# Merging the experts' lists on 64 rows of batch and expert, in parts around the last block's gate

## The chip, the cores and the metric

One core of a Trainium2 chip runs one program that holds an attention layer and a layer of experts (MoE). The metric is the time of the program on the device in microseconds, the median of several executions. Nothing else runs on the core.

## What is computed

The input x has two batches of 2048 tokens with 256 features (float32). The reference is, cut to what matters here:

```python
x = x + attention(layernorm(x))      # 16 heads, segments of 64 tokens, a memory carried over segments
h = layernorm(x)                     # all 4096 tokens of both batches in one list
scores = sigmoid(h @ gate_w.T)       # 32 experts; 4 groups of 8, the best 2 groups stay
topk_idx, topk_w = best 4 of (scores + gate_bias) within those groups, weights normalised, times 2
# expert e takes the first CAP = 64 tokens that chose it, in the order of the list
h1 = silu(buf @ w1) * (buf @ w3);  ob = h1 @ w2
y = sum over the kept choices of weight * ob
x = x + y + shared(h)                # a shared expert on all tokens
```

The point for this change is the capacity. Of the 4096 tokens, each expert keeps only the 64 that come first. The kernel finds them as the 64 largest of a list: for each expert a row holds, at a token's place, N minus its number if the token chose the expert and 0 if not. The largest values are the earliest tokens.

## The kernel before, in words

The attention part goes through 16 blocks (`NBLK`) of 128 tokens of both batches, and in each through 4 groups (`NG`) of 4 heads. The order of the work on each engine is written out by hand, engine by engine, with semaphores between them; an engine works its own list strictly in that order. While block n + 1 is in attention, the rows of block n are finished: the output projection (`project_out`, L1591), the residual (`residual`, L1033), the second layer norm (`x1_stats`, `x1_newton`, `x1_apply`, L921 to L946), the transposes of the normed rows (`x1_transposes`, L1601), the logits (`logits`, L1609), the gate on VectorE (`gate_scores` to `gate_weights`, L1055 to L1114), the transposes of the picks (`pick_transposes`, L1615) and their product with the descending numbers `desc` (`picks`, L1119 to L1135), which yields for every expert a row of 128 values for each batch.

The rows of the first 14 blocks go out to memory and come back as `first_picks`: 128 rows (batch, half, expert) of 896 columns. `earliest` (L1142, L1143) takes the 64 largest of each of those rows in eight rounds. A round is one MAX8, which finds the eight largest of a row, and one MATCH_REPLACE8, which puts -1 in their places. Its result `first_kept` is four lists of 64 for each expert.

After the last block of attention the rest of the lists is merged on VectorE:

- The four lists of `first_kept` are copied side by side into `mid` (L1300), on 32 rows (one for each expert), and SP is told (`lists_kept`). Behind them lie the picks of block 15, both batches: 4 x 64 + 2 x 128 = 512 columns. `picks(15)` puts them there in two instructions (L1126), one for each batch.
- Eight rounds of `top8` (L1201, L1202) put the 64 largest of the 512 into the first 64 columns of `last_picks`.
- Then comes the last block: residual, layer norm, gate, picks. `picks(16)` puts its rows behind them: 64 + 256 = 320 columns.
- Eight rounds of `top8` on the 320 columns give `sel`, the final list. Between the rounds stand some sums of the shared expert (`shared_add`, L1195, and `shared_mul`, L1189).
- Three small steps (L1335 to L1339) make token numbers of it. TensorE turns them (`pair_tokens`, L1674), VectorE makes the indices (L1341), and POOL (GpSimd) gathers the experts' tokens with them (L653), stores and broadcasts the list to all partitions (L646, L676).

TensorE fills this stretch with the shared expert. Its order after the attention is:

```python
        attended_transposes(NT - 1)
        project_out(NBLK, NT)
        shared_half(0, 1, 0)
        shared_half(0, 1, 1)
        x1_transposes(NBLK)
        logits(NBLK)
        shared_down(0)
        shared_up(1, 0)
        pick_transposes(NBLK)
```

and then `shared_up(1, 1)`, `shared_up(2, 0)`, `shared_down(1)`, `shared_up(2, 1)`, `shared_up(3, 0)`, `pair_tokens`, `shared_down(2)`, `shared_up(3, 1)`, `shared_down(3)` and the expert loop. `shared_up` is L1648, `shared_down` L1667. `shared_down(g)` waits for the two `shared_mul(g, ..)` on VectorE. SP (SyncE) issues most transfers: in this stretch the return of the rows of blocks 1 to 12, six batches of expert weights (L477, L480), the store of the last block's rows (L446), two more batches, the store of its columns. ScalarE makes the exponentials for the gate (L837) and the shared expert's silu (L848).

Of the kernel before, what the change touches and what calls it, by code (L numbers as in the profile page):

```python
# [10 lines left out]
ALU = mybir.AluOpType  # L11
# [4 lines left out]
B, S, D = 2, 2048, 256  # L16
H, DK = 16, 128
SEG = 64
BLK = 2 * SEG
NBLK = S // BLK  # L20
# [5 lines left out]
E, F, FS = 32, 128, 256  # L26
# [5 lines left out]
CAP = 2 * (256 * TOPK // E)  # L32
# [36 lines left out]
def layer(nc, ctx, io, scratch, out):  # L69

    def sb(name, shape, dt=fp32):
        return ctx.enter_context(nc.sbuf_tensor(name, shape, dt))

    def sem(name):
        return ctx.enter_context(nc.semaphore(name))
# [22 lines left out]
    HB = HG // 2  # L98
    WR, WC = 8, 2

    def carve(region):

        at = [0]

        def take(shape, dt=fp32):
            size = math.prod(shape[1:])
            t = region[0:shape[0], at[0]:at[0] + size]
            at[0] += size
            if dt != fp32:
                t = t.bitcast(dt)  # L110
            dims = "abcde"[:len(shape) - 1]
            return t if len(shape) == 2 else t.rearrange(
                "p (%s) -> p %s" % (" ".join(dims), " ".join(dims)),
                **dict(zip(dims, shape[1:])))
        return take
# [23 lines left out]
    toks = take([128, E, CAP])  # L139
# [11 lines left out]
    first_kept = shared_place[:, NG * 3 * NC * HG * DK + PART:NG * 3 * NC * HG * DK + PART + CAP]  # L151


    flat_toks = toks[0:E, :, :].rearrange("p e c -> p (e c)")
    at = 4 * CAP + B * BLK
    mid, last_picks = flat_toks[:, 0:at], flat_toks[:, at:at + CAP + B * BLK]
    hits = take([128, NP])
    target = take([128, 3, NP])
    oidx = take([128, NP], u32)
# [15 lines left out]
    at = B * (D + ROW)  # L175
# [64 lines left out]
    desc = sb("desc", [B * E, BLK])  # L240
# [9 lines left out]
    def bank(name):  # L250
        return ctx.enter_context(nc.psum_tensor(name, [128, 512], fp32))
# [4 lines left out]
    bank_a, bank_v = bank("bank_a"), bank("bank_v")  # L256
# [22 lines left out]
    s = {n: sem(n) for n in names}  # L279
# [5 lines left out]
    s2 = {n: sem("p2_" + n) for n in names2}  # L285
# [7 lines left out]
    ROUNDS = CAP // 8  # L293
# [259 lines left out]
    def _(pool):  # L553
# [88 lines left out]
        pool.wait_ge(s2["last_row_stored"], 16)  # L642
        pool.wait_ge(s["zeroed"], 16 * (NBLK + 1))

        pool.wait_ge(s2["top_step"], 4 * ROUNDS + 3)
        pool.dma_start(scratch["toks"], idxf[:, 2, :]).then_inc(s2["toks_stored"], 16)  # L646

        def gather(p):
# [258 lines left out]
    def _(dve):  # L907
# [136 lines left out]
        def x1_apply(blk):  # L1044
            dve.wait_ge(s["row_stored"], 16 * blk)
            norm_apply(ln_x1, xrow, x1, "x1_normed")

        def gate_link(blk, before):
            return link_on(dve, s["gate_step"], (blk - 1) * GATE_STEPS + before, s["dve_noted"])

        def gate_scores(blk):

            dve.wait_ge(s["lg_exp"], blk)
            link, v = gate_link(blk, 0), nc.vector
            link(v.tensor_scalar_add(eg[:, :, :], eg[:, :, :], 1.0))  # L1055
            link(v.reciprocal(score[:, :, :], eg[:, :, :]))
            link(v.tensor_tensor(scb[:, :, :], score[:, :, :], gbias[:, :, :], ALU.add), True)
# [48 lines left out]
        def gate_weights(blk):  # L1106

            link, v = gate_link(blk, PICK_STEP), nc.vector
            link(v.tensor_tensor(wsel[:, :, :], score[:, :, :], pick[:, :, :], ALU.mult))
            link(v.tensor_reduce(wsum[:, 0, :], wsel[:, :, :], axis=AX.X, op=ALU.add))  # L1110
            link(v.tensor_scalar_add(wsum[:, 1, :], wsum[:, 0, :], 1e-20))
            link(v.reciprocal(wsum[:, 2, :], wsum[:, 1, :]))
            for b in range(B):
                ins = v.tensor_scalar(xrow[:, b, D:ROW], wsel[:, b, :], wsum[:, 2, b:b + 1], 2.0,  # L1114
                                      ALU.mult, ALU.mult)
            link(ins)

        def picks(blk):

            dve.wait_ge(s["pickt_mm"], blk)  # L1120
            dve.wait_ge(s["desc_ready"], B + blk - 1)
            if blk >= NBLK - 1:
                to = mid[:, 4 * CAP:] if blk < NBLK else last_picks[:, CAP:]
                for b in range(B):
                    e = slice(b * E, (b + 1) * E)
                    ins = nc.vector.tensor_tensor(to[:, b * BLK:(b + 1) * BLK], bank_a[e, 0:BLK],  # L1126
                                                  desc[e, :], ALU.mult)
                ins.then_inc(s["pickv_ready"], 1)
            else:
                dve.wait_ge(s["pickv_stored"], 16 * B * (blk - 1))  # L1130
                nc.vector.tensor_tensor(pickv, bank_a[0:B * E, 0:BLK],
                                        desc[:, :], ALU.mult).then_inc(s["pickv_ready"], 1)
            if blk < NBLK:
                dve.wait_ge(s["pickv_ready"], blk + 1)
                nc.vector.tensor_scalar_add(desc[:, :], desc[:, :], -float(BLK)  # L1135
                                            ).then_inc(s["desc_ready"], 1)
# [28 lines left out]
        link = link_on(dve, s["bt_ready"], 0)  # L1165
# [18 lines left out]
        def shared_mul(g, fc):  # L1184
            dve.wait_ge(s2["sil_ready"], FC * g + fc + 1)
            dve.wait_ge(s2["u_mm"], FC * g + fc + 1)
            if g:
                dve.wait_ge(s2["d_mm"], TG * g)
            nc.vector.tensor_tensor(sh[:, fc, :], sil[:, fc, :], bank_u[fc][:, :], ALU.mult  # L1189
                                    ).then_inc(s2["sh_ready"], 1)  # L1190
# [6 lines left out]
        link = link_on(dve, s2["top_step"], 0)  # L1197

        def top8(out, values, r):

            link(nc.vector.max(out[:, 8 * r:8 * r + 8], values))  # L1201
            link(nc.vector.match_replace(out=values, in_to_replace=out[:, 8 * r:8 * r + 8],  # L1202
                                         in_values=values, imm_value=-1.0))
# [4 lines left out]
        def body(blk, first, last):  # L1208
            for g in range(NG):
# [74 lines left out]
                if g == 3 and not first:  # L1284
                    gate_weights(blk)
                    picks(blk)
# [10 lines left out]
        earliest(ROUNDS)  # L1297
        dve.wait_ge(s["list_step"], 2 * ROUNDS)
        for q in range(4):
            ins = nc.vector.tensor_copy(mid[:, q * CAP:(q + 1) * CAP],  # L1300
                                        first_kept[q * E:(q + 1) * E, :])
        ins.then_inc(s["lists_kept"], 1)
        shared_mul(0, 0)
        dve.wait_ge(s["pickv_ready"], NBLK)
        dve.wait_ge(s["lists_kept"], 1)
        for r in range(ROUNDS):
            top8(last_picks, mid, r)
        residual(NBLK)
        x1_stats(NBLK)
        x1_newton(NBLK, 0, NEWTONS)  # L1310
        x1_apply(NBLK)
        shared_mul(0, 1)
        gate_scores(NBLK)
        gate_group_sums(NBLK)
        gate_groups(NBLK)
# [1 line left out]
        gate_top(NBLK)  # L1317
        gate_picks(NBLK)
        gate_weights(NBLK)
        picks(NBLK)  # L1320
        shared_mul(1, 0)
        dve.wait_ge(s["pickv_ready"], NBLK + 1)
# [131 lines left out]
    def _(pe):  # L1454
# [167 lines left out]
        for c in range(NC):  # L1622
            ins = nc.tensor.transpose(bank_s[:, c * E:(c + 1) * E], gw[:, c * 128:(c + 1) * 128],
                                      ident[0:E, 0:E])
# [44 lines left out]
                ins.then_inc(s2["d_mm"], 1)  # L1669

        def pair_tokens():
            pe.wait_ge(s2["top_step"], 4 * ROUNDS + 3)
            for h in range(2):
                ins = mm(bank_t[HALF[h], 0:NP], idxf[:, 2, :], ident[0:E, h:E:2], start=True, stop=True)  # L1674
            ins.then_inc(s2["sel_mm"], 1)
# [211 lines left out]
```

## Time and profile before

| | us |
|---|---|
| median of 3 executions | 1669.26 (1668.77 to 1669.92) |
| the profiled execution | 1669.3 |
| its span in the trace | 1667.5 |
| TensorE busy | 1623.2 |
| VectorE busy | 1143.7 |
| ScalarE busy | 884.9 |
| GpSimd busy | 497.9 |
| mean granted TensorE clock, share of full speed | 0.993 |

Times of the trace are microseconds from the start of the span. A number behind L is the line of the kernel. "Busy" means that an instruction of the engine ran; the idle time before an instruction stands in brackets with what ended it. The attention part ends near 1500, the expert loop runs from about 1571 to 1620, and the rest is the shared expert of the later blocks and the output.

### The profile page before, as it was taken

Reading aid. Unit: us, or ns where it says so; the run is one execution under the profiler, and the core shown is the slowest. Engines: PE = TensorE matmul, PEld = TensorE weight load, DVE = VectorE, ACT = ScalarE, POOL = GpSimd, SP = SyncE. Lnnn points to the kernel's source line nnn. Section 1 sums busy time; section 2 is a strip of 40 time slices with the busy share of each in tenths; the row PEclk is TensorE's granted clock in tenths of the full one; section 3 lists DMA queues with packets and bytes.
Section 4 is the critical chain, followed back from the end, with each engine's and each line's share of the span. In section 5 each row is a group of like instructions: output and inputs, shape, how many; then the busy total and the mean of one; then the engine's idle time right before and its main releaser. Section 6 shows DMA issues by size and latency. Waiting matters only on the chain.

```text
span 1667.5 us, 42642 instructions
## 1 busy us (share of the span) xinstructions
PE 1623.2 (97%) x17190; PEld 1418.9 (85%) x17190; DVE 1143.7 (69%) x3508; ACT 884.9 (53%) x1955; POOL 497.9 (30%) x438
## 2 busy tenths in 40 slices
PE   6899999999999999999999999999999999997998
PEld 5798999899998989998999989998999989875555
DVE  6865858586775757575776758585867757688544
ACT  5664646465563646364654646464655636451131
POOL 2332323232332313231333323232323323130351
PEclk9999999999999999999999999999999999998999
DMA  5102121212202121212112021212011021228847
GB/s 183 49 21 77 35 78 33 79 30 58 58 29 85 34 71 33 86 33 68 38 44 74 29 77 36 77 33 79 31 57 58 29 88 34 73 97 263 266 90 215
DMA packets 121780, 122.06 MB, mean 73 GB/s; under 512 B 24032, under 2 KB 101296, under 8 KB 121456
## 3 DMA queue, kind: packets, MB, share of 16 engines
q1 hardware_dynamic: 118224, 113.52, 22.3%
q0 software_dynamic: 3328, 5.81, 1.8%
q8 instruction: 136, 2.23, 0.6%
q14 instruction: 60, 0.49, 0.1%
q10 hardware_dynamic: 32, 0.01, 0.0%
HBM read 94.90 MB, written 24.40 MB: 72 GB/s over the span
## 4 chain that ended last, share of the span: by engine, by line
PE 93%; DVE 5%; issue 1%; ACT 1%; DMA 0%; DVEq 0%; ACTq 0%
PE bank_p L1473 23%; PE bank_v L1591 13%; PE chain_k L1546 6%; PE chain_k L1524 6%; PE bank_a L1481 5%; PE bank_v L1481 5%; PE chain_q L1524 5%; PE bank_s L1494 4%; PE chain L1524 3%; PE bank_a L1562 3%; PE bank_p L1504 3%; PE bank_p L1648 2%; PE bank_v L1573 2%; PE bank_a L1573 2%; PE bank_s L1579 2%; PE chain L1546 2%
## 5 line engine op out<-in xcount | busy, mean ns | idle before, releaser
L588 POOL TENSOR_TENSOR step_place<-step_place 128x512 f32<-128x512 f32 x128 | 166.7, 1303 | 575.5 <-ACT step_place L734 426.5
L756 ACT ACTIVATE step_place<-chain_q,step_place 128x128 f32<-128x128 f32 x384 | 113.3, 368 | 225.3 <-DVE step_place L990 225.3
L1591 PE MATMUL bank_v<-step_place 128*128 128x256 f32 x1024 | 225.3, 381 | 0.7 <-ACT step_place L767 0.7
L1473 PE MATMUL bank_p<-xt_hi,w_hi 128*128 128x256 f32 x1024 | 220.0, 296 | 4.6 <-DVE w_lo L911 2.5
L1591 PEld LDWEIGHTS bank_v<-step_place 128*128 128x128 f32 x1024 | 193.2, 190 | 29.2 <-issue 2.6
L1473 PE MATMUL bank_p<-xt_hi,w_lo 128*128 128x256 f32 x1024 | 206.6, 283 | 0.0
L1473 PE MATMUL bank_p<-xt_lo,w_hi 128*128 128x256 f32 x1024 | 206.4, 283 | 0.0
L625 POOL TENSOR_TENSOR step_place<-step_place 128x512 f32<-128x512 f32 x64 | 69.4, 1084 | 433.2 <-DVE step_place L1251 433.2
L1473 PEld LDWEIGHTS bank_p<-xt_hi,w_hi 128*128 128x128 f32 x1024 | 158.4, 191 | 24.0 <-issue 14.5
L978 DVE SCALAR_TENSOR_TENSOR step_place<-step_place,bank_p 128x512 f32<-128x512 f32 x128 | 87.5, 684 | 109.3 <-ACT bank_p L728 109.2
L1473 PEld LDWEIGHTS bank_p<-xt_hi,w_lo 128*128 128x128 f32 x1024 | 160.0, 192 | 0.0
L1473 PEld LDWEIGHTS bank_p<-xt_lo,w_hi 128*128 128x128 f32 x1024 | 159.5, 192 | 0.0
L595 POOL TENSOR_TENSOR step_place<-step_place 128x512 f32<-128x512 f32 x128 | 150.0, 1192 | 0.0
L734 ACT ACTIVATE step_place<-bank_a 128x512 f32<-128x512 f32 x64 | 39.3, 614 | 205.7 <-PE bank_a L1481 205.7
L1033 DVE TENSOR_TENSOR rows_place<-bank_v,turned 128x512 f32<-128x512 f32 x16 | 11.1, 691 | 173.3 <-PE bank_v L1591 173.2
L1546 PE MATMUL chain_k<-step_place 64*128 64x129 f32 x762 | 118.5, 288 | 0.2 <-ACT step_place L822 0.2
L1546 PE MATMUL chain_q<-step_place 64*128 64x129 f32 x762 | 118.6, 288 | 0.0
L1546 PEld LDWEIGHTS chain_k<-step_place 64*128 64x128 f32 x762 | 94.2, 187 | 20.0 <-issue 19.3
L999 DVE SCALAR_TENSOR_TENSOR step_place<-chain_k,step_place 128x128 f32<-128x128 f32 x381 | 110.5, 346 | 0.7 <-issue 0.6
L1524 PE MATMUL chain_k<-step_place 128*64 128x129 f32 x1536 | 110.9, 279 | 0.0
L741 ACT ACTIVATE step_place<-bank_p 128x512 f32<-128x512 f32 x128 | 69.5, 596 | 75.9 <-PE bank_s L1546 75.9
L1524 PE MATMUL chain_q<-step_place 128*64 128x129 f32 x1536 | 106.4, 272 | 0.0
(219 smaller groups left out, 3959.8 us busy)
## 6 DMA issues: line engine op xcount, KB each, us to landing
step_place<-in_L_attn_Wo_dram SPq DMA_DIRECT2D x128, 256.0 KB, 2.7
step_place<-beta_all SPq DMA_DIRECT2D x64, 256.0 KB, 3.4
expert_place<-in_L_ffn_w_dram SPq DMA_DIRECT2D x24, 512.0 KB, 7.6
expert_sums<-zero SPq DMA_DIRECT2D x16, 272.0 KB, 4.9
expert_rows<-rows_place SPq DMA_DIRECT2D x15, 288.0 KB, 2.3
step_place<-in_L_attn_x_dram SPq DMA_DIRECT2D x16, 256.0 KB, 3.9
turned<-in_L_attn_x_dram SPq DMA_DIRECT2D x16, 256.0 KB, 3.9
x_rows<-rows_place SPq DMA_DIRECT2D x16, 256.0 KB, 2.8
```

What stands on the lines that cost most here:

```text
L588: nc.gpsimd.tensor_tensor(dl[seg][:, :, 0:DK], val[:, seg, :, :], beta_rows[:, :, :], ALU.mult).then_inc(s["vb_ready"], 1)
L595: nc.gpsimd.tensor_tensor(vo[:, seg, :, :], val[:, seg, :, :], dl[seg][:, :, 0:DK], ALU.subtract).then_inc(s["vo_ready"], 1)
L625: nc.gpsimd.tensor_tensor(sm[:, :, :], sm[:, :, :], sinv[:, :].unsqueeze(2).to_broadcast([128, T, SEG]), ALU.mult).then_inc(s["p_ready"], 1)
L741: nc.scalar.activation(ksig[:, HB * h:HB * h + HB, :, :].rearrange("p j s d -> p (j s d)"), bank_p[h][:, :], ACT.Copy).then_inc(s["ksig_re ...
L756: ins = nc.scalar.activation(to[:, j, :], t[:, at:at + DK], ACT.Copy, scale=rd[:, seg, r:r + 1])
L978: nc.vector.scalar_tensor_tensor(out=t, in0=t, scalar=1.0, in1=bank_p[h][:, :], op0=ALU.min, op1=ALU.add).then_inc(s["k_sig"], 1)
L999: ins = nc.vector.scalar_tensor_tensor(out=dl[seg][:, j, 0:DK], in0=t[:, at:at + DK], scalar=rd[:, seg, j:j + 1], in1=dl[seg][:, j, 0:DK], ...
L1473: ins = mm(out, w[:, g, m, c, col], x[:, c, :, :].rearrange("p s t -> p (s t)"), start=i == 0, stop=i == len(parts) - 1)
L1481: ins = mm(seg_bank[seg][:, :], x[:, c, seg, :], w[:, g, 2, c, :], start=i == 0, stop=i == len(parts) - 1)
L1524: ins = mm(t[ROWS[half], at:at + ZC], sig[:, j, seg, b, :], mem[:, HG * g + j, b, :], start=True, stop=True)
L1546: ins = mm(change(b, j), ksig[ROWS[b], j, seg, :], dl[seg][ROWS[b], j, :], start=True, stop=True)
L1591: ins = mm(bank_v[:, b * D:(b + 1) * D], att[:, b * PIECES + i, :], wo[:, i % WR, :], start=(i == 0 and b == 0), stop=(i == PIECES - 1), s ...
```

## The change

The last but one merge runs on 64 rows, one for each batch and expert, with 2 x 64 kept values and the 128 picks of block 15: 256 columns in place of 512. `picks(15)` is therefore one instruction. The eight rounds are split: `MID_FIRST` = 4 of them ahead of the residual of the last block, three between `shared_mul(0, 1)` and `gate_scores`, and one behind `gate_weights`, ahead of the last block's picks. They leave two lists for each expert, one for each batch; two copies bring them side by side into `last_picks`, which has 2 x 64 + 256 = 384 columns in place of 320. The link behind the copies adds one to the count that POOL and TensorE wait for.

```diff
+    MID_FIRST, MID_THEN = 4, 7
...
-    flat_toks = toks[0:E, :, :].rearrange("p e c -> p (e c)")
-    at = 4 * CAP + B * BLK
-    mid, last_picks = flat_toks[:, 0:at], flat_toks[:, at:at + CAP + B * BLK]
+    flat_toks = toks[:, :, :].rearrange("p e c -> p (e c)")
+    at = 2 * CAP + BLK
+    mid, mid_kept = flat_toks[0:B * E, 0:at], flat_toks[0:B * E, at:at + CAP]
+    at += CAP
+    last_picks = flat_toks[0:E, at:at + B * CAP + B * BLK]
...
-        pool.wait_ge(s2["top_step"], 4 * ROUNDS + 3)
+        pool.wait_ge(s2["top_step"], 4 * ROUNDS + 4)
...
-            if blk >= NBLK - 1:
-                to = mid[:, 4 * CAP:] if blk < NBLK else last_picks[:, CAP:]
+            if blk == NBLK - 1:
+                nc.vector.tensor_tensor(mid[:, 2 * CAP:], bank_a[0:B * E, 0:BLK], desc[:, :], ALU.mult
+                                        ).then_inc(s["pickv_ready"], 1)
+            elif blk == NBLK:
+                to = last_picks[:, B * CAP:]
                 for b in range(B):
...
         for q in range(4):
-            ins = nc.vector.tensor_copy(mid[:, q * CAP:(q + 1) * CAP],
+            b, part = divmod(q, 2)
+            ins = nc.vector.tensor_copy(mid[b * E:(b + 1) * E, part * CAP:(part + 1) * CAP],
                                         first_kept[q * E:(q + 1) * E, :])
         ins.then_inc(s["lists_kept"], 1)
         shared_mul(0, 0)
         dve.wait_ge(s["pickv_ready"], NBLK)
         dve.wait_ge(s["lists_kept"], 1)
-        for r in range(ROUNDS):
-            top8(last_picks, mid, r)
+
+        for r in range(MID_FIRST):
+            top8(mid_kept, mid, r)
         residual(NBLK)
         x1_stats(NBLK)
         x1_newton(NBLK, 0, NEWTONS)
         x1_apply(NBLK)
         shared_mul(0, 1)
+        for r in range(MID_FIRST, MID_THEN):
+            top8(mid_kept, mid, r)
         gate_scores(NBLK)
...
         gate_weights(NBLK)
+        for r in range(MID_THEN, ROUNDS):
+            top8(mid_kept, mid, r)
+        for b in range(B):
+            ins = nc.vector.tensor_copy(last_picks[:, b * CAP:(b + 1) * CAP],
+                                        mid_kept[b * E:(b + 1) * E, :])
+        link(ins)
         picks(NBLK)
...
         def pair_tokens():
-            pe.wait_ge(s2["top_step"], 4 * ROUNDS + 3)
+            pe.wait_ge(s2["top_step"], 4 * ROUNDS + 4)
```

## Rows read from the trace of the kernel before

**Rows 1.** The page, busy time of each engine, its share and instructions.
```profile
PE 1623.2 (97%) x17190; PEld 1418.9 (85%) x17190; DVE 1143.7 (69%) x3508; ACT 884.9 (53%) x1955; POOL 497.9 (30%) x438
```
**Rows 2.** The chain that ended last: start, length, engine, what it wrote, line.
```profile
1510.95 0.69 DVE shared_place L1201
...
1522.88 0.70 DVE rows_place L1033
...
1531.66 3.56 PE bank_s L1667 x8
```
**Rows 3.** Timeline of TensorE: start, length, line, operation, count, idle before.
```profile
1501.76 14.08 PE L1591 MATMUL bank_v<-step_place 128*128 128x256 f32 x64 [0.69 <-ACT step_place L767]
...
1517.40 1.88 PE L1648 MATMUL chain_q<-shared_place 128*128 128x512 f32 x4
1527.94 1.12 PE L1601 MATMUL bank_v<-ident,rows_place 128*128 128x128 f32 x4 [8.67 <-DVE rows_place L946]
1529.75 1.91 PE L1609 MATMUL bank_a<-gwt,turned 128*128 128x32 f32 x8 [0.69 <-ACT turned L842]
...
1540.22 0.27 PE L1615 MATMUL bank_a<-ident,pick 128*64 128x128 f32 x1
...
1547.20 1.89 PE L1667 MATMUL bank_s<-shared_place 128*128 128x256 f32 x8
...
1557.61 0.29 PE L1674 MATMUL chain<-ident,shared_place 32*64 32x16 f32 x4
1559.62 1.97 PE L1667 MATMUL bank_s<-shared_place 128*128 128x256 f32 x8 [1.72 <-DVE shared_place L1195]
```
**Rows 4.** Timeline of VectorE, the same columns.
```profile
1497.16 0.57 DVE L1126 TENSOR_TENSOR shared_place<-bank_a,desc 32x128 f32<-32x128 f32 x2
...
1509.54 0.77 DVE L1300 COPY shared_place<-shared_place 32x64 f32<-32x64 f32 x4
...
1531.95 0.20 DVE L1055 TENSOR_SCALAR eg<-eg 128x64 f32<-128x64 f32 x1 [3.47 <-ACT eg L837]
...
1538.18 0.39 DVE L1114 TENSOR_SCALAR rows_place<-wsel,wsum 128x32 f32<-128x32 f32 x2
1540.59 0.57 DVE L1126 TENSOR_TENSOR shared_place<-bank_a,desc 32x128 f32<-32x128 f32 x2 [2.02 <-issue]
...
1546.27 0.69 DVE L1189 TENSOR_TENSOR shared_place<-shared_place,chain_q 128x512 f32<-128x512 f32 x1
...
1547.96 0.48 DVE L1201 MAX8 shared_place<-shared_place 32x8 f32<-32x320 f32 x1
...
1549.05 0.48 DVE L1201 MAX8 shared_place<-shared_place 32x8 f32<-32x320 f32 x1
...
1553.42 0.18 DVE L1339 TENSOR_SCALAR shared_place<-shared_place 32x64 f32<-32x64 f32 x1
1558.02 0.17 DVE L1341 CAST shared_place<-chain 128x16 uint32<-128x16 f32 x1 [4.42 <-PE chain L1674]
...
1575.42 0.33 DVE L1357 COPY shared_place<-shared_place 64x2 f32<-64x2 f32 x2
```
**Rows 5.** VectorE's groups by form, 1500 to 1560: count, busy us, mean ns.
```profile
L1142 DVE MAX8 shared_place<-shared_place 128x8 f32<-128x896 f32 x4 | 4.4, 1092 | 0.1
```
**Rows 6.** The picks of the other blocks, line 1131: shortest, median and longest in ns.
```profile
L1131 DVE TENSOR_TENSOR rows_place<-bank_a,desc x14: 281/282/283, 205.5 to 1409.4; 64x128 f32<-64x128 f32 x14
```
**Rows 7.** Timeline of SP's transfers: start, length of the issue, line, transfer.
```profile
1548.43 0.85 SPq L446 DMA_DIRECT2D x_rows<-rows_place  x1
```
**Rows 8.** Stretches: length, busy per engine, granted clock, DMA share, GB/s.
```profile
1521.00:1522.00 1.00, 0.00 (x0) 0.00 (x0) 0.96 (x2) 0.00 (x0) 0.00 (x0) 0.71 1.16 326
...
1572.00:1576.00 4.00, 3.86 (x29) 2.17 (x31) 1.94 (x7) 1.90 (x6) 0.00 (x0) 1.00 0.27 106
```
**Rows 9.** Transfers issued 1470 to 1600: size, us to landing.
```profile
expert_rows<-rows_place POOLq DMA_DIRECT2D x1, 288.0 KB, 6.4
```
**Rows 10.** Timeline of POOL: start, length of the issue, line, transfer.
```profile
1561.59 0.59 POOL L676 DMA_DIRECT2D shared_place<-expert_tokens  x1
```

## The prediction

> **The bound.** I read the page first: TensorE is busy for 97% of the span [rows 1], so a change on VectorE can only pay where TensorE stands still. Then the chain of waits over the last 270 us, to see where the end hangs on something else. It leaves TensorE for VectorE in one long piece: the eight rounds of the last but one merge, from 1510.95 to the residual of the last block at 1522.88, then the layer norm up to 1527.94 where TensorE takes over again [rows 2, 3]. Then TensorE's timeline: the output projection starts at 1501.76 and takes 14.08, the two shared halves behind it end at 1519.28, and the transposes of the last block wait 8.67 us for VectorE [rows 3]. That hole is what the change is about. From 1529.75 TensorE runs through shared work without a break up to `pair_tokens` at 1557.61 [rows 3], while VectorE has the final list ready at 1553.60 and waits 4.42 us for those four small matmuls [rows 4]. So in that stretch the end hangs on TensorE's queue, which starts as early as the last block's normed rows allow. All times are of one profiled execution of 1669.3 us (span 1667.5); the median of the runs shown is 1669.26, so a difference taken from the trace can be taken from either.
>
> **A round.** Eight rounds on 32 rows of 512 took 1522.88 - 1510.95 = 11.93, 1.491 each [rows 2]. A round on 320 columns took 1549.05 - 1547.96 = 1.09 [rows 4]. Slope 0.401 / 192 = 2.09 ns a column for both passes. So 256 columns cost 0.96 and 384 cost 1.22. That 64 rows cost no more than 32 is what the pass over 128 rows of 896 says: 1.092 us [rows 5]. The passes on 32 rows, 0.48 for 320 columns and 0.69 for 512 [rows 2, 4], give 0.48 + 576 x 1.09 ns = 1.11 for as many.
>
> **Part 1.** The picks of the block before the last: two instructions on 32 rows (0.57 together, [rows 4]) become one on 64 rows, whose like in the other blocks takes 0.28 [rows 6]. TensorE waits for exactly this semaphore before its last `attend`, so that, the sums behind it and the projection come 0.28 earlier: the projection ends at 1515.84 - 0.28 = 1515.56.
>
> **Part 2.** Four rounds ahead of the residual in place of eight. The merge starts at 1510.95 - 0.28 = 1510.67 and four rounds of 0.96 end at 1514.5. The residual also needs the projection, 1515.56. So the rounds are no longer what it waits for; the projection is late next, and about 1 us of the saving is lost to it. The residual starts at about 1515.62, 7.26 earlier; the normed rows are ready 5.06 later as before (1527.94 - 1522.88), at 1520.68. TensorE is done with the shared halves at 1519.0 by then: the hole of 8.67 becomes 1.7.
>
> **Part 3.** Three rounds behind `shared_mul(0, 1)`. VectorE waited 3.47 us there for the exponentials [rows 4]. Three rounds cost 2.87, from 1515.62 + 5.6 = 1521.2 to 1524.1. The cover is the way over TensorE and ScalarE: 4.01 from the transposes to `gate_scores` (1531.95 - 1527.94), that is 1524.7 if it goes as before. They cost nothing, with 0.6 to spare. If that way ran at full clock it would end some 0.9 earlier and the rounds would hold the gate by 0.3.
>
> **Part 4.** The last round and two copies ahead of the picks: 0.96, and two copies of 0.19 with their link, 0.42 (four took 0.77, [rows 4]): 1.38. Before, VectorE stood 2.02 us here, since the pick transposes lay behind `shared_up(1, 0)` in TensorE's queue [rows 3, 4]. The gate takes 6.62 (1531.95 to 1538.57), so 1524.7 + 6.62 + 1.38 = 1532.7, while the transposes come at 1520.68 + 12.28 = 1533.0 (1540.22 - 1527.94). Hidden, by 0.3 us. The pick mask is made ahead of the weights, so TensorE finds it in time.
>
> **Part 5.** The last merge on 384 columns for 320: eight rounds at 0.133 more: 1.07. The list is late by that, but VectorE had 4.42 us in hand against `pair_tokens`. One thing sits inside: `shared_mul(1, 1)` comes after three rounds, 5.68 behind the picks and now 6.08, and `shared_down(1)` waits for it. Before, it was done just before TensorE came (1546.27 + 0.69 against 1547.20). Now 1533.33 + 6.08 + 0.69 = 1540.1 against 1520.68 + 19.26 = 1539.94: a new wait of 0.16.
>
> **Queues.** SP's queue holds the store of the last block's rows behind six batches of expert weights; it was issued at 1548.43, 25 us after its rows were there [rows 7], so earlier rows change nothing on it. `lists_kept` comes 0.28 earlier. POOL's store of the gate rows and its gathers move up with the gate and the list; they are then issued while SP's weights fill the DMA engines. The store of 288 KB that was issued in such a stretch landed after 6.4 us [rows 9], against 13.8 us between the issue of the tokens' broadcast and the first work behind its wait (1561.59 to 1575.42, [rows 4, 10]). The broadcast of the tokens moves from 1561.59 to about 1554 [rows 10] and is wanted at 1575.42 - 8 = 1567.4 [rows 4]. I cost the transfers at nothing; without that cover they are the second and third rival.
>
> **The clock.** In the hole of before the granted clock fell from 2.4 to 1.2 GHz inside 1521 to 1522 (a mean of 0.71 between 1 and 0.5, so at about 1521.4), some 2.1 us after the last matmul [rows 8]. A hole of 1.72 us before 1559.62 left it at full [rows 3]. The new hole is 1.7, then 0.5 of transposes, then 0.65 for ScalarE's copy: between those two rows. If the clock falls there as before, the sums above hold: the shift is 7.26 - 0.16 = 7.1, a little more since the transposes themselves still run at full clock (up to 0.5, of which about 0.1 reaches the end). I take 7.2.
> If it doesn't fall, TensorE's part from transposes to picks is shorter by 3.3: 1.83 on the first half of `shared_down(0)` (3.56 for 1.73, [rows 2, 3]), 0.95 on the logits, 0.5 on the transposes. Then VectorE leads: 1524.1 + 6.62 + 1.38 = 1532.1 for the picks, 1538.85 for `shared_mul(1, 1)`, while TensorE was ready at 1536.6; `pair_tokens` at 1538.85 + 10.41 = 1549.26, 8.35 earlier.
> The Trainium skill (TensorE: Matmul & The Clock Gate, on HAM oscillation) warns only of gaps longer than either new one, so by it the clock stays and the sum is 8.35; the fall in [rows 8] came sooner after the last matmul than that lets one expect, so I weigh it as a rival and not as the forecast.
>
> **Sum.** 1669.3 - 7.2 = 1662.1. What follows `pair_tokens` (idle slots, gathers, the expert loop, the closing shared groups) hangs on that point and keeps its length.
>
> **Rivals.**
> First, full clock throughout: 1669.3 - 8.35 = 1660.95. For it speaks the 1.72 hole at full clock; against it two holes in close order at the first place, and a wait of 1538.85 - 1536.6 = 2.2 at `shared_down(1)`, as long as the time after which the clock fell before. If it falls only there, 3.4 to 6.8 us at half clock cost 1.7 to 3.4 with nothing to hide it: 1662.65 to 1664.35.
> Second, transfers take over: the first gathers or the tokens, now among the weights, are late for the expert loop. The 8 us by which POOL's issues come earlier all fall into the stretch of the weights; if half of that is lost again, the expert loop starts 4 us later than forecast: near 1666. Against it: what POOL issued among the weights landed in 6.4.
> Third, on the other side, one mechanism: POOL's queue gets no share of the engines until all that SP has queued is through, near 1573, where the DMA share falls from full to 0.27 [rows 8]. A transfer like the 6.4 us one then ends at 1579.4 against 1575.4 for its use before, 4.0 later: 1673.3. It decides against the change once the broadcast lands after 1575.4. [Rows 9] speak against it.
> Fourth, the change doesn't do what it says: the residual is held by the projection far longer, or ScalarE's exponentials keep their old distance from something else. Then 0 to 4 us of gain. I see no such thing: both transfers that the residual waits for were long done.
>
> **Chances.** Mechanism with one fall of the clock early, 1662.1: 0.48. Full clock: 0.22. Fall at the second place only: 0.17. Transfers partly in the way: 0.06. Slower by starved transfers: 0.02. Little or nothing gained: 0.05. The range must hold 0.8: from 1660.3 (full clock, with 0.6 for my rounding and the runs' own spread of 1.15) to 1664.4 (the later fall at its longest). A measurement of this kernel tells 0.2%, 3.3 us, from no change. Faster by more: the first three cases and part of the fourth, 0.92; within: 0.06; slower: 0.02.
>
> **Signs.** The residual right behind the end of the projection near 1515.6; the transposes near 1520.7 with a wait of 1.7 for VectorE; three rounds of 0.96 between `shared_mul` and `gate_scores` with at most a short wait behind; picks near 1532 to 1533; the rounds of the last merge at 1.22; a new wait at `shared_down(1)`, short at half clock, 2.2 at full; `pair_tokens` between 1549.2 and 1550.5. It is wrong if the 64-row rounds cost over 1.2 each, if the residual starts well behind the projection, or if a gather or the tokens end the wait ahead of the expert loop.

## The result, and the profile after

The changed kernel takes 1663.10 us in the median of 6 executions (1662.24 to 1664.63), the kernel before 1669.01 (1668.22 to 1669.92). The ratio is 0.9965 with a 95% interval of 0.9952 to 0.9978: 5.9 us faster, or 0.35%. The forecast of 1662.1 was 1.0 us too low (7.2 us of gain for 5.9), inside its range; in part that was luck, as the section on the prediction says.

| | before | after |
|---|---|---|
| profiled execution | 1669.3 | 1663.68 |
| its span | 1667.5 | 1661.9 |
| TensorE busy | 1623.2 | 1622.4 |
| VectorE busy | 1143.7 | 1140.1 |
| mean granted clock | 0.993 | 0.997 |

The lines of the file have moved: on TensorE, L1608 is now the output projection, L1618 the transposes of the last block, L1626 the logits, L1632 the pick transposes, L1665 `shared_up`, L1684 `shared_down`, L1691 `pair_tokens`. On VectorE, L1208 and L1209 are `top8`, L1037 the residual, L1196 `shared_mul`.

The timeline of TensorE after the change (start, length, line, operation, count, idle before), to be laid beside [rows 3]:

```profile
1496.81 0.27 PE L1632 MATMUL bank_a<-ident,pick 128*64 128x128 f32 x1
...
1502.23 15.77 PE L1608 MATMUL bank_v<-step_place 128*128 128x256 f32 x64 [0.69 <-ACT step_place L771]
...
1523.16 0.65 PE L1618 MATMUL bank_v<-ident,rows_place 128*128 128x128 f32 x4 [1.74 <-DVE rows_place L950]
1524.51 1.08 PE L1626 MATMUL bank_a<-gwt,turned 128*128 128x32 f32 x8 [0.69 <-ACT turned L846]
...
1532.39 0.27 PE L1632 MATMUL bank_a<-ident,pick 128*64 128x128 f32 x1
...
1541.46 1.99 PE L1684 MATMUL bank_s<-shared_place 128*128 128x256 f32 x8 [1.93 <-DVE shared_place L1196]
...
1551.97 0.29 PE L1691 MATMUL chain<-ident,shared_place 32*64 32x16 f32 x4
```

Three things are to be seen. The hole of 8.67 us ahead of the last block's transposes is 1.74. There is a new one of 1.93 ahead of `shared_down(1)`, put down to `shared_mul(1, 1)` on VectorE. And the projection, the same 64 matmuls, takes 15.77 us where it took 14.08.

The timeline of VectorE after the change, beside [rows 2, 4]:

```profile
1497.85 0.28 DVE L1127 TENSOR_TENSOR shared_place<-bank_a,desc 64x128 f32<-64x128 f32 x1
...
1511.42 0.41 DVE L1208 MAX8 shared_place<-shared_place 64x8 f32<-64x256 f32 x1
...
1512.38 0.42 DVE L1208 MAX8 shared_place<-shared_place 64x8 f32<-64x256 f32 x1
...
1518.09 0.69 DVE L1037 TENSOR_TENSOR rows_place<-bank_v,turned 128x512 f32<-128x512 f32 x1 [2.84 <-PE bank_v L1608]
...
1526.52 0.20 DVE L1059 TENSOR_SCALAR eg<-eg 128x64 f32<-128x64 f32 x1
...
1534.13 0.48 DVE L1334 COPY shared_place<-shared_place 32x64 f32<-32x64 f32 x2
1534.64 0.57 DVE L1133 TENSOR_TENSOR shared_place<-bank_a,desc 32x128 f32<-32x128 f32 x2
...
1540.71 0.69 DVE L1196 TENSOR_TENSOR shared_place<-shared_place,chain_q 128x512 f32<-128x512 f32 x1
...
1542.54 0.55 DVE L1208 MAX8 shared_place<-shared_place 32x8 f32<-32x384 f32 x1
...
1543.77 0.55 DVE L1208 MAX8 shared_place<-shared_place 32x8 f32<-32x384 f32 x1
...
1552.38 0.17 DVE L1358 CAST shared_place<-chain 128x16 uint32<-128x16 f32 x1 [3.67 <-PE chain L1691]
```

A round on 64 rows of 256 columns takes 1512.38 - 1511.42 = 0.96, one on 384 columns 1543.77 - 1542.54 = 1.23: as forecast. The residual now waits 2.84 us for the projection. The exponentials' wait of 3.47 and the picks' wait of 2.02 are gone (no bracket): VectorE works without a pause from the residual to the end of the list. It still waits 3.67 for `pair_tokens`.

The granted clock in the stretch of the projection, after and then before (columns: length, busy of PE, PEld, DVE, ACT, POOL, granted clock, DMA share, GB/s):

```profile
1503.00:1504.00 1.00, 1.00 (x3) 0.75 (x3) 0.97 (x2) 0.00 (x0) 0.00 (x0) 0.50 0.00 0
1504.00:1506.00 2.00, 2.00 (x6) 1.58 (x5) 1.93 (x4) 0.00 (x0) 0.00 (x0) 0.50 0.00 0
1507.00:1508.00 1.00, 1.00 (x6) 0.87 (x6) 0.97 (x2) 0.00 (x0) 0.00 (x0) 1.00 0.59 195
```

```profile
1503.00:1506.00 3.00, 3.00 (x16) 2.64 (x15) 2.93 (x4) 0.00 (x0) 0.00 (x0) 1.00 0.28 87
```

Between 1503 and 1506 eight matmuls ran (the two windows count one of them twice) where sixteen ran before, at 1.2 GHz and not 2.4. In windows of half a microsecond the clock is at half from about 1502.7 to 1506.2; half of these 3.4 us is lost, which is the 1.69. The matmuls and the holes ahead of them are those of the kernel before, but for 0.2 us.

**Where the 5.6 us of span come from.** Four points that both traces have: the pick transposes of block 15, the start of the projection, the residual, `pair_tokens`.

| from, to | before | after | gain | forecast at full clock |
|---|---|---|---|---|
| start of span to pick transposes | 1496.12 | 1496.81 | -0.69 | 0 |
| to the projection | 5.64 | 5.42 | 0.22 | 0.28 |
| to the residual | 21.12 | 15.86 | 5.26 | 6.98 |
| to `pair_tokens` | 34.73 | 33.88 | 0.85 | 1.09 |
| to the end of the span | 109.89 | 109.93 | -0.04 | 0 |
| sum | | | 5.60 | 8.35 |

The forecast of 7.2 took -0.06 and not 1.09 in the fourth line (the new wait of 0.16, with some 0.1 back), since it placed the fall of the clock there. The first line is not the change's doing: the attention part is the same work in both.

### The profile page after: what moved, and what is told of

Same layout as the page of the kernel before. It is cut to its first block, busy times and chain, and to the rows that moved or that the text cites. A ratio compares the mean times of both kernels' runs of the same rounds, so it can differ in the third digit from the quotient of the medians.

```text
span 1661.9 us, 42644 instructions
## 1 busy us (share of the span) xinstructions
PE 1622.4 (98%) x17190; PEld 1417.8 (85%) x17190; DVE 1140.1 (69%) x3509; ACT 884.0 (53%) x1955; POOL 497.8 (30%) x438
## 4 chain that ended last, share of the span: by engine, by line
PE 93%; DVE 5%; issue 1%; ACT 1%; DMA 0%; DVEq 0%; ACTq 0%
PE bank_p L1490 23%; PE bank_v L1608 14%; PE chain_k L1563 6%; PE chain_k L1541 6%; PE bank_a L1498 5%; PE bank_v L1498 5%; PE chain_q L1541 5%; PE bank_s L1511 4%; PE bank_a L1579 3%; PE chain L1541 3%; PE bank_p L1521 3%; PE bank_a L1590 2%; PE bank_v L1590 2%; PE bank_s L1596 2%; PE chain L1563 2%; PE bank_p L1665 1%
## 5 line engine op out<-in xcount | busy, mean ns | idle before, releaser
L1608 PE MATMUL bank_v<-step_place 128*128 128x256 f32 x1024 | 227.0, 383 | 0.7 <-ACT step_place L771 0.7
L1608 PEld LDWEIGHTS bank_v<-step_place 128*128 128x128 f32 x1024 | 194.4, 191 | 29.7 <-issue 2.6
L1037 DVE TENSOR_TENSOR rows_place<-bank_v,turned 128x512 f32<-128x512 f32 x16 | 11.1, 692 | 176.1 <-PE bank_v L1608 176.1
```

The source lines that it names most:

```text
L1608: ins = mm(bank_v[:, b * D:(b + 1) * D], att[:, b * PIECES + i, :], wo[:, i % WR, :], start=(i == 0 and b == 0), stop=(i == PIECES - 1), s ...
```

## The experiments

Twelve kernels, in three groups of four. The kernel before ran beside each group, with medians of 1669.54, 1669.33 and 1669.22, and 1669.01 beside the changed kernel. Ratios are to the kernel before. Where kernels of different groups are compared by their medians, a difference of 0.5 us or less says nothing.

**The rounds in parts, without the 64-row form.**

The edit is on the kernel before.

```diff
-        for r in range(ROUNDS):
+        for r in range(3):
             top8(last_picks, mid, r)
...
         shared_mul(0, 1)
+        for r in range(3, 5):
+            top8(last_picks, mid, r)
         gate_scores(NBLK)
...
         gate_weights(NBLK)
+        for r in range(5, ROUNDS):
+            top8(last_picks, mid, r)
         picks(NBLK)
```

> The kernel before with its 32 rows of 512 columns, and only the eight rounds split: three ahead of the residual, two ahead of gate_scores, three behind gate_weights. If the hole on TensorE is what counts and VectorE's path to the picks is next: the residual follows the projection, about 7.0 us earlier than before; the three rounds of 1.49 behind the weights then hold the picks to 1535.6, shared_mul(1, 1) is done at 1542.0, pair_tokens near 1552.4 to 1552.9, that is 4.7 to 5.2 us faster than before. Rival (the narrow form does the work, the split little): less than 2 us faster.

Measured: 1665.37 (11 executions), ratio 0.9979 (0.9970 to 0.9988), 4.2 us faster. The residual came 0.55 us behind its turn, ended by the projection; the hole ahead of the transposes was 1.73, and `pair_tokens` came at 1553.20, 4.4 earlier. A little under what was expected, and far from the rival's 2. In this profile the clock was at half from 1522.6 to 1529.3, behind the hole.

**The 64-row form, with all rounds ahead of the residual.**

```diff
-    MID_FIRST, MID_THEN = 4, 7
+    MID_FIRST, MID_THEN = 8, 8
```

> The changed kernel with all eight rounds of the 64-row merge ahead of the residual. Rounds of 0.96 end at 1518.4, the residual starts 4.5 us earlier than before, the hole on TensorE is about 4.2 and the clock falls in it as before; 4.3 us faster than before. Rival (the split alone counts): equal to before within 1 us.

Measured: 1664.70 (8 executions), 0.9973 (0.9963 to 0.9984), 4.8 us faster. So each half of the change gets most of the gain by itself, and the two overlap: either one takes most of the hole away. Its residual came at 1519.09 with no wait ahead of it, and the hole was 2.80 where 4.2 was expected: its projection, too, took 15.77 us in the profile, so TensorE came to the hole 1.7 later. Behind the hole the clock fell a second time, to half from 1526.2 to 1529.7; from the transposes to the picks it took 10.91 us, 1.7 more than in the changed kernel.

**Five rounds first, three in the gap, none behind the weights.**

```diff
-    MID_FIRST, MID_THEN = 4, 7
+    MID_FIRST, MID_THEN = 5, 8
```

> The changed kernel with five rounds ahead of the residual and three ahead of gate_scores, none behind the weights. If the projection is what the residual waits for, the fifth round is free, and the picks come one round (0.96) earlier where VectorE leads: 0.3 to 1.0 us faster than the changed kernel, so 6.2 to 6.9 faster than before. Rival (the residual waits for the rounds): 0 to 1 us slower than the changed kernel.

Measured: 1662.87 (1661.72 to 1664.93, 5 executions), 0.9961 (0.9947 to 0.9974). That is 6.7 us faster than before and 0.2 faster than the changed kernel by the medians, which is not to be told from nothing. Its profiled execution was a slow one (1664.93), and for two reasons. It came to the pick transposes of block 15 at 1498.40, 1.6 us later than the changed kernel's, in work that is the same. And it has what the forecast had placed there, a fall of the clock behind the first hole:

```profile
1523.38 1.00 PE L1618 MATMUL bank_v<-ident,rows_place 128*128 128x128 f32 x4 [2.05 <-DVE rows_place L950]
1525.07 1.91 PE L1626 MATMUL bank_a<-gwt,turned 128*128 128x32 f32 x8 [0.69 <-ACT turned L846]
1526.80 3.73 PE L1684 MATMUL bank_s<-shared_place 128*128 128x256 f32 x8
...
1535.52 0.27 PE L1632 MATMUL bank_a<-ident,pick 128*64 128x128 f32 x1
```

From the transposes to the picks it took 12.14 us (1535.52 - 1523.38), as in the kernel before (12.28, [rows 3]); in the changed kernel's profile it was 9.23. VectorE then waited 1.52 us for the pick transposes, and the saved round was lost in that wait. From the pick transposes of block 15 to the end of the span it took 164.7 us, the changed kernel 165.1. The fifth round itself was free: the residual still waited 0.19 us for the projection.

**Filling TensorE's hole in the kernel before.** Matmuls whose results nobody reads, ahead of `x1_transposes`, keep the engine busy; here 18 of 512 columns.

```diff
+        pe.wait_ge(s2["sil_ready"], 1)
+        idle_matmuls(18, bank_p[0])
         x1_transposes(NBLK)
```

> The kernel before with 18 matmuls of 512 columns, whose results nobody reads, in TensorE's hole of 8.67 us ahead of the last block's transposes. If the half clock behind the hole costs what the forecast says (3.3 us on TensorE, of which VectorE's rounds give back 0.3), pair_tokens comes 3.0 us earlier and the kernel is about 3 us faster than before. Rival (the clock costs nothing here, since VectorE leads): no change, or slower by up to 0.5 us if the added matmuls overrun the hole.

Measured: 1672.69, 1.0021 (1.0012 to 1.0030), 3.2 us slower. The edit was miscounted: a matmul of 512 float32 columns is two instructions of 0.43 us each, so the 18 took 15.6 us and held the transposes 6.9 us longer than in the kernel before (1534.80 against 1527.94). Still it says what was asked: from the transposes to `pair_tokens` 1561.36 - 1534.80 = 26.56 us, where the kernel before took 29.67.

Then 19 of 256 columns:

```diff
+        idle_matmuls(19, bank_p[0])
```

> The kernel before with 19 matmuls of 256 columns (0.43 us each at full clock, 8.2 us together) in TensorE's hole of 8.67, the run before this having overrun it by 6.9. Theory (the half clock behind the hole costs about 3 us): 3.0 us faster than before, granted clock full between 1520 and 1540. Rival: the overrun hid nothing and the kernel is within 0.5 us of before.

Measured: 1667.75 (11 executions), 0.9987 (0.9978 to 0.9996), 1.6 us faster: half of the 3.0. In the trace the full 3.0 are there. The matmuls fit in (a wait of 0.48 us for VectorE was left), and from the transposes to `pair_tokens` 26.62 us passed, 3.05 less than before:

```profile
1521.60 8.37 PE L1655 MATMUL bank_p<-shared_place 128*128 128x256 f32 x38
1530.45 0.66 PE L1601 MATMUL bank_v<-ident,rows_place 128*128 128x128 f32 x4 [0.48 <-DVE rows_place L946]
...
1557.07 0.29 PE L1678 MATMUL chain<-ident,shared_place 32*64 32x16 f32 x4
```

But this execution was 2.5 us later than that of before already at the pick transposes of block 15 (1498.61 against 1496.12), in work that is the same in both. Those 2.5 us arose in the first 50. TensorE waited 3.23 us for VectorE at 32.86 (0.22 before), and behind that wait the clock was at half from 32 to 39, where before it was at full (this kernel, then the kernel before):

```profile
32.00:39.00 7.00, 6.14 (x30) 5.92 (x32) 4.08 (x11) 3.44 (x9) 1.04 (x1) 0.51 0.90 305
32.00:39.00 7.00, 6.03 (x57) 5.70 (x56) 4.67 (x15) 5.74 (x13) 1.05 (x1) 1.00 0.78 248
```

The eleven executions fall in two groups: five at 1665.71 to 1666.65, with a mean granted clock of 0.997 or 0.998, and six at 1667.75 to 1668.83, the profiled one among them, with 0.996 or 0.997. The first group is about 3 us faster than before. That the whole second group lost its time in the same early place is likely and not shown, since one execution alone was profiled.

**Filling the holes of the changed kernel.**

```diff
+                if g == 3 and last:
+                    pe.wait_ge(s2["sil_ready"], 1)
+                    idle_matmuls(2, bank_p[0])
...
+        idle_matmuls(1, bank_p[0])
         attended_transposes(NT - 1)
+        idle_matmuls(1, bank_p[0])
         project_out(NBLK, NT)
...
+        idle_matmuls(3, bank_p[0])
         x1_transposes(NBLK)
+        idle_matmuls(1, bank_p[0])
         logits(NBLK)
...
         shared_up(2, 0)
+        idle_matmuls(4, chain_3)
         shared_down(1)
```

> The changed kernel with short matmuls of 256 columns, whose results nobody reads, in every hole of TensorE from the last attend to shared_down(1): 2, 1, 1, 3, 1 and 4 of them, 0.43 us each. Theory (what separates the measured 1663.1 from the 1660.95 of the full clock is a fall of the clock in one of these holes, at a place that differs from run to run): about 2 us faster than the changed kernel, 1661.0, and the output projection takes 14.1 and not 15.8. Rival (the missing 1 to 2 us went elsewhere, into transfers or the ends of the span): within 0.5 us of the changed kernel.

Measured: 1662.89 (1662.50 to 1663.32), 0.9960 (0.9947 to 0.9974). A miss: nothing gained on the changed kernel's 1663.10. The projection did take 14.08 us again, and `pair_tokens` came at 1549.93, 2.0 earlier. Then the clock fell behind the first hole that wasn't filled, the one of 1.71 behind `pair_tokens`, and the whole of it was given back (1661.5 - 1496.47 = 165.0 us from the pick transposes of block 15 to the end, as in the changed kernel):

```profile
1550.00:1552.00 2.00, 0.29 (x5) 0.22 (x5) 1.67 (x5) 0.00 (x0) 0.60 (x1) 1.00 1.13 334
1552.00:1554.00 2.00, 2.00 (x6) 1.60 (x7) 0.39 (x1) 0.00 (x0) 1.70 (x3) 0.64 1.11 359
1554.00:1556.00 2.00, 2.00 (x6) 1.64 (x5) 0.00 (x0) 0.00 (x0) 1.56 (x2) 0.50 1.24 307
```

Two more fills, three short matmuls behind `pair_tokens` and two ahead of `shared_down(3)`, tell whether that is the reason.

> The changed kernel with the holes filled as in e6_clock_kept, and two more behind it: three short matmuls behind pair_tokens and two ahead of shared_down(3). Theory (e6_clock_kept gained nothing because the clock then fell in the next hole, behind pair_tokens): no fall between 1495 and 1570, 1661.0, which is 1.9 us faster than e6_clock_kept. Rival (keeping the clock is worth nothing to the end, something else absorbs it): 1662.9 again.

Measured: 1662.07 (1660.93 to 1662.17), 0.9955 (0.9942 to 0.9969): 0.8 us faster than without the two and 1.0 faster than the changed kernel, where 1.9 was expected. Its trace has no fall between 1495 and 1570, and between pick transposes and end of span it took 1660.4 - 1496.96 = 163.4 us, against 165.1 in the changed kernel and 171.4 before. So the clock accounts for 1.7 of the changed kernel's profiled execution, and for about 1 in the medians. The slowest of its executions (1662.17) is just below the fastest of the changed kernel (1662.24), but the intervals of the two ratios overlap.

**`shared_mul(1, 1)` earlier.**

```diff
             top8(sel, last_picks, r)
+            if r == 0:
+                shared_mul(1, 1)
             if r < 2:
                 shared_add(0, r)
-            if r == 2:
-                shared_mul(1, 1)
```

> The changed kernel with shared_mul(1, 1) behind the first round of the last merge and not behind the third. Theory (VectorE leads from the residual to shared_down(1) at full clock, and that wait of 1.93 goes straight to the end): 1.9 us faster than the changed kernel where the clock stays full, nothing where it falls early; 1.0 to 1.9 in the median, near 1661.5. Rival (pair_tokens is bound by something later, the end of the list): no change.

Measured: 1661.30 (1658.54 to 1661.39), 0.9947 (0.9934 to 0.9961), 1.8 us faster than the changed kernel, whose executions it doesn't overlap. Its profile has the same fall in the projection (15.77 us), full clock behind it, and no wait at `shared_down(1)`:

```profile
1518.24 0.69 DVE L1037 TENSOR_TENSOR rows_place<-bank_v,turned 128x512 f32<-128x512 f32 x1 [2.84 <-PE bank_v L1608]
```

```profile
1539.52 1.89 PE L1684 MATMUL bank_s<-shared_place 128*128 128x256 f32 x8
...
1549.93 0.29 PE L1691 MATMUL chain<-ident,shared_place 32*64 32x16 f32 x4
```

From residual to `pair_tokens` 31.69 us, 2.19 less than in the changed kernel. The hole ahead of `shared_down(3)`, too, was back from 1.19 to 0.84. From the pick transposes of block 15 to the end it took 162.5 us for 165.1: the wait that the change made had been paid in full at the end of the kernel.

**That and five rounds first.**

> The changed kernel with shared_mul(1, 1) behind the first round and five rounds ahead of the residual, three ahead of gate_scores; nothing filled. TensorE is bound by its own work from the transposes on, so the earlier picks add nothing: equal to e7_mul_earlier within 0.5 us, 1661.3. Rival (each of the two steps pays by itself): 1660.4.

Measured: 1661.83 (1660.75 to 1662.94), 0.9956 (0.9943 to 0.9970), 0.5 us slower than with `shared_mul` moved alone, where the rival wanted it faster. By itself that is no clean test, since here the clock fell behind the hole of 2.05 us ahead of the transposes and cost more there (below). The clean one is at full clock: from the transposes to `pair_tokens` TensorE took 26.62 us with four rounds first (1549.93 - 1523.31, `shared_mul` moved alone) and 26.62 with five (1548.19 - 1521.57, the next one). The earlier picks add nothing, as expected.

**All together: five rounds first, `shared_mul` earlier, the holes up to the logits filled.**

> Both together, with five rounds ahead of the residual and three ahead of gate_scores, and with the holes filled (2, 1, 1, 3 and 1 short matmuls; the wait at shared_down(1) should be gone). If clock and shared_mul are what is left, TensorE is bound by its own work from the transposes on: 1659.0, 4 us faster than the changed kernel, 10 faster than before. Rival (the two overlap): 1661, no better than the better of the two alone.

Measured: 1659.29 (1658.87 to 1659.52), 0.9939 (0.9925 to 0.9952), 10.0 us faster than before and 3.8 faster than the changed kernel, whose executions it doesn't overlap. In its profile the residual waited 0.18 us for the projection and started at 1516.18, and `pair_tokens` came at 1548.19, 32.01 later. With the two later holes filled too:

> As e8_all_three with the two later holes filled too. The profile of that run had no fall of the clock in this stretch already: the same time, 1659.2 to 1659.3, within 0.4 us. Rival (most of its executions had a fall behind pair_tokens): 1 to 1.7 us faster, 1657.6 to 1658.3.

Measured: 1659.53 (1659.29 to 1660.60), 0.9943 (0.9929 to 0.9956). No further gain; a fall behind `pair_tokens` wasn't what most executions of that kernel had.

**The picks in two instructions again.**

```diff
-                nc.vector.tensor_tensor(mid[:, 2 * CAP:], bank_a[0:B * E, 0:BLK], desc[:, :], ALU.mult
-                                        ).then_inc(s["pickv_ready"], 1)
+                for b in range(B):
+                    e = slice(b * E, (b + 1) * E)
+                    ins = nc.vector.tensor_tensor(mid[e, 2 * CAP:], bank_a[e, 0:BLK],
+                                                  desc[e, :], ALU.mult)
+                ins.then_inc(s["pickv_ready"], 1)
```

> The changed kernel with the picks of block 15 in two instructions of 32 rows again. From the pick transposes to the start of the output projection 5.64 us as in the kernel before (5.42 in the changed one). Forecast of the 0.28: if it were whole, the changed kernel would show 5.36. Rival (the 0.22 comes from elsewhere): 5.42 stays.

Measured, in one execution: 1662.97, beside the 1663.10 of the changed kernel. From the pick transposes to the projection 1501.84 - 1496.20 = 5.64 us, as in the kernel before. In the changed kernel it is 5.42, and 5.41 or 5.42 in all eight other profiled kernels with the single instruction. The step is worth 0.22 us, and not the 0.28 by which the instruction is shorter.

## Why the prediction was right, and where it was off

**The bound and the hole** were read rightly. TensorE's queue from the transposes on sets the end, and the change pays by closing the hole ahead of them: 8.67 to 1.74 us (1.7 forecast). Each half of the change alone closes most of it (to 1.73 and 2.80) and is worth 4.2 and 4.8 us.

**The cost of a round** by a slope between two rows held: 0.96 and 1.23 (0.96 and 1.22 forecast), so the 64 rows cost nothing that the slope from 32 rows doesn't give.

**Part 1**: 0.22 for 0.28, shown by the run that undoes it.

**Part 2**: the projection is late next, as said; the residual waited 2.84 us for it in the profile, and 1.15 or 1.16 in the three runs with four rounds in which the projection kept its 14.08. The fifth round is therefore free, which the run with five showed (0.19 left).

**Parts 3 and 4** came out as in the case of the full clock: three rounds held the gate by a few tenths, and the last round and the copies held the picks. The copies took 0.51 with their link for 0.42. From the residual to the picks 16.55 us, 16.48 forecast.

**Part 5**: the wait at `shared_down(1)` was 1.93 (2.2 forecast for the full clock, 0.16 for the forecast's own case). It was shown to cost what it lasts, 1.8 us in the medians.

**The transfers** stayed covered. The list of transfers of the changed kernel, 1470 to 1600 (KB, us from issue to landing):

```profile
shared_place<-expert_tokens POOLq DMA_DIRECT2D x1, 1024.0 KB, 9.4
expert_rows<-rows_place POOLq DMA_DIRECT2D x1, 288.0 KB, 6.3
```

The tokens' broadcast, issued at 1555.96 among the weights, was there at 1565.4, ahead of its use at 1570.14, and the store of 288 KB took 6.3 for the 6.4 of [rows 9]. So the second and third rival are out. From `pair_tokens` to the end it took 109.93 us, 109.89 before. One small thing was missed: `shared_down(3)` waited 1.19 us and not 0.84.

**The clock** is the step that failed, in its place and not in its kind. The forecast placed one fall behind the hole ahead of the transposes and took 1.1 us for it. In the profiled execution the clock stayed at full there and fell at the start of the projection, in work that the change hardly touches, where the forecast had no term: 1.69 us, all of it on the path. The right sum for that execution is 8.35 - 1.72 for the projection - 0.69 for the attention part, which ended later in it - 0.24 between residual and `pair_tokens` - 0.06 in part 1 - 0.04 behind = 5.60, which is what was measured. That 7.2 came near the measured 5.9 is in part luck: a fall that the forecast had booked at 1.1 didn't come there, and one that it had not booked cost 1.7. The profiles show a fall in the projection (the changed kernel, the 64-row form alone, `shared_mul` earlier), behind the hole ahead of the transposes (each half alone, both kernels with five rounds and nothing filled), behind `pair_tokens` (the first filling, the two picks), or nowhere in this stretch (the second filling, and both versions with everything). The 64-row form alone is named twice, since it fell at both places in one execution. The falls came behind holes of 0.69 to 2.80 us, and which one the fall takes differs between executions of nearly the same work; why is not shown.

What a fall costs differs with how long the clock stays down. In the projection (half clock from 1502.7 to 1506.2) it was 1.7, in `shared_down(2)` too, and in the 64-row form alone, where it came only at the start of `shared_down(0)` (1526.2 to 1529.7). In three other profiles it came earlier behind the hole ahead of the transposes, among the transposes and the small matmuls of the logits. With five rounds first it was down for twice as long (1523.5 to 1530.4), and transposes to picks took 12.14 us for 9.23. With `shared_mul` moved and five rounds first, residual to `pair_tokens` took 34.93 us with the fall and 32.01 without (the runs with nothing filled and with everything): again 2.9, near the 3.3 that the forecast had for TensorE. Behind the long hole of the kernel before it was 3.0; there the clock was back only at 1535, seven us after work had begun:

```profile
1535.00:1536.00 1.00, 1.00 (x6) 0.87 (x5) 0.75 (x5) 0.00 (x0) 0.00 (x0) 0.96 1.10 345
```

The Trainium skill (TensorE: Matmul & The Clock Gate, on HAM oscillation) warns only of gaps longer than the holes of 0.69 to 2.80 us behind which the clock fell here; falls behind holes of 1.71 and 2.05 us don't agree with it as a rule for a single gap, and the measurement decides. The forecast's own sum of 8.35 for a clock that stays was met by the profile from the residual on (33.88 against 33.64 to `pair_tokens`).

What the forecast should have done is to price one fall somewhere in the stretch, at 1.7 at least, and take it off the full-clock sum: 8.35 - 1.7 = 6.65, against the 5.9 of the medians. Of the 0.75 that is left, 0.3 stands in the small terms above; the rest is open. It had this number only as a rival for the wait at `shared_down(1)`.

## What to carry to other kernels

Where a second engine hands work to the engine that bounds, look for that engine's long hole and for the work ahead of the hand-over that could wait; put it where the second engine idles anyway. Then ask at once which instruction of the second engine the bound engine meets next: here a multiply queued behind three rounds cost 1.9 us that moving one line got back. When holes shrink from long to short, don't book the clock as saved: price at least one fall for the whole stretch, wherever it may come (one of the profiles here had two).

## What the runs showed that was not expected

- The clock fell behind short holes in close order: in the changed kernel at about 1502.7 behind holes of 1.30, 0.80 and 0.69 us with small matmuls between them. The kernel before has the same holes within 0.1 us (1.39, 0.93 and 0.69) and kept the full clock in its profiled execution. Of the ten profiles in which these holes were not filled three fell in the projection, of the four in which they were none did.
- With idle matmuls in six holes the clock fell behind the seventh, and nothing was gained (1662.89 against 1663.10). That the filling moved the fall is not shown: with none filled and the picks in two instructions it fell behind the same hole. Filling that one and the one ahead of `shared_down(3)` too gained 0.8 us.
- The same attention part ended between 1495.9 and 1498.6 (by the pick transposes of block 15) in the profiled executions of these kernels. A difference of 1 to 2 us between two single executions of this kernel can lie wholly there. The two latest (1498.61 and 1498.40) were 2.7 us late already at about 50 us, behind a wait of over 3 us for VectorE and with the half clock that followed it.
- A matmul of 512 float32 columns is listed as two instructions of 0.43 us, one of 256 columns as two of 0.22.
